# Local attention in a two-layer network on one NeuronCore: the stages of a step put one step apart, and the value products in a bank per block parity

## The reference, cut to what matters

```python
qkv = x @ Wqkv                               # 16 heads of 64
q = l2norm(q) * qs ; k = l2norm(k) * ksc
q = q * cos * scale + rotate_half(q) * sin * scale
k = k * cos * inv + rotate_half(k) * sin * inv
sim = einsum('bhwie,bhwje->bhwij', bq, bk2) * QK_SCALE   # windows of 32, each sees itself and the one before
attn = softmax(where(mask, -max, sim), -1)
out = einsum('bhwij,bhwje->bhwie', attn, bv2)
x = x + out @ Wo
...
a, gate = split(layernorm(x) @ W1 + b1, 2)
x = x + (a * gelu(gate)) @ W2 + b2
```

## Time and profile before

| | us |
|---|---|
| median of 3 runs | 6201.04 (6194.84 to 6217.79) |
| the profiled execution's own time | 6205.79 |
| its span, first to last instruction | 6204.0 |
| PE busy | 5057.0 (82%) |
| DVE busy | 3565.5 (57%) |
| ACT busy | 3480.0 (56%) |
| POOL busy | 2018.9 (33%) |
| mean granted TensorE clock | 0.892 of full speed |

### The profile page before, as it was taken

How to read it: one execution, slowest core, us unless ns; L and a number is a source line. 1 busy time by engine, 2 the same in 40 slices (tenths; PEclk the granted TensorE clock), 3 DMA queues, 4 the chain that set the end, 5 groups by cost and what they waited for, 6 DMA issues and landing times. The chain is left out here.

```text
span 6204.0 us, 161424 instructions
## 1 busy us (share of the span) xinstructions
PE 5057.0 (82%) x63808; PEld 2746.5 (44%) x63808; DVE 3565.5 (57%) x5172; ACT 3480.0 (56%) x10701; POOL 2018.9 (33%) x1438
## 2 busy tenths in 40 slices
PE   7888887777767888888888888888888888888887
PEld 3333333222224445545554455445545544554453
DVE  5677666333335556655666566555656565665564
ACT  3444444233225666666666666666666666666665
POOL 2122211000004444444444444344444444444441
PEclk9999998777678999999999999998999999999998
DMA  1000000000013233333333333333333333333332
GB/s 40 0 0 0 0 0 21 0 0 0 0 58 75 66 70 70 81 81 71 70 74 83 73 71 73 77 79 69 71 70 88 76 69 70 76 85 70 70 70 79
DMA packets 197293, 340.19 MB, mean 55 GB/s; under 512 B 63568, under 2 KB 63568, under 8 KB 195024
## 3 DMA queue, kind: packets, MB, share of 16 engines
q1 hardware_dynamic: 196560, 330.14, 22.5%
HBM read 34.19 MB, written 6.29 MB: 7 GB/s over the span
## 5 line engine op out<-in xcount | busy, mean ns | idle before, releaser
L376 ACT ACTIVATE c_Pb<-c_S,c_nb 128x64 f32<-128x64 f32 x3072 | 914.4, 323 | 477.9 <-DVE c_nb L665 476.4
L342 POOL TENSOR_TENSOR c_F<-c_tAB 128x1024 f32<-128x1024 f32 x384 | 905.9, 2359 | 8.8 <-DVE c_tAB L646 8.5
L646 DVE SCALAR_TENSOR_TENSOR c_tAB<-c_PA,c_WP,c_base 128x1024 f32<-128x1024 f32 x384 | 492.9, 1284 | 662.1 <-ACT c_sq L361 652.7
L330 POOL TENSOR_TENSOR c_Pb<-c_Pb,c_rs 128x512 f32<-128x512 f32 x384 | 400.0, 1042 | 1449.1 <-DVE c_rs L673 1449.1
L334 POOL TENSOR_TENSOR c_sq<-c_sq 128x512 f32<-128x512 f32 x384 | 486.6, 1267 | 1068.3 <-ACT c_sq L361 1068.3
L661 DVE COPY c_VO<-c_PB 128x512 f32<-128x512 f32 x384 | 265.2, 691 | 938.3 <-PE c_PB L479 938.3
L470 PE MATMUL c_PD<-c_sq,c 128*128 128x512 f32 x768 | 525.6, 773 | 332.7 <-DVE c_F L653 323.1
L376 ACT ACTIVATION_READ_ACCUMULATOR c_Pb<-c_S,c_nb 128x1 f32 x3072 | 665.9, 217 | 0.0
L519 PE MATMUL c_S<-c_PTs,c_VE 64*64 64x32 f32 x10752 | 442.8, 224 | 207.7 <-DVE c_PTs L679 198.9
L519 PEld LDWEIGHTS c_S<-c_PTs,c_VE 64*64 64x64 f32 x10752 | 404.8, 139 | 366.3 <-issue 366.3
L389 ACT ACTIVATE c_OT<-c_S 64x256 f32<-64x256 f32 x1536 | 542.8, 377 | 23.2 <-PE c_S L519 10.5
(11 more groups left out here) (247 smaller groups left out, 9515.2 us busy)
## 6 DMA issues: line engine op xcount, KB each, us to landing
c_QK<-c_F SPq DMA_DIRECT2D x3072, 64.0 KB, 2.0
c_VE<-c_VO SPq DMA_DIRECT2D x384, 128.0 KB, 2.6
c_VE<-c_VO SPq DMA_DIRECT2D x384, 96.0 KB
c_stage<-in_w_heads SPq DMA_DIRECT2D x24, 256.0 KB, 4.2
c_WT<-in_w_tails SPq DMA_DIRECT2D x6, 1024.0 KB, 5.9
a_W<-in_w_level SPq DMA_DIRECT2D x1, 3335.5 KB, 10.6
c_WT<-in_w_tails SPq DMA_DIRECT2D x6, 537.5 KB, 3.7
b_W<-in_w_level SPq DMA_DIRECT2D x1, 3133.0 KB, 10.2
```

The costliest lines, as they stand in the source:

```text
L330: nc.gpsimd.tensor_tensor(p, p, rs[:, n % 2, :].unsqueeze(2).broadcast_to([P, HS, KEYS]), ALU.mult).then_inc(*p_ready.up())
L342: nc.gpsimd.tensor_tensor(F[:, j % 2], tAB[:, j % 2, 0], tAB[:, j % 2, 1], ALU.add).then_inc(*rotated.up())
L376: e = nc.scalar.activation(Pb[:, n % 2, i, :], S[:, n % 2, r, c * KEYS:(c + 1) * KEYS], ACT.Exp, bias=nb[:, n % 2, r * PS + c:r * PS + c + ...
L646: nc.vector.scalar_tensor_tensor(out=tAB[:, kind, half], in0=bank[:, :].unsqueeze(1).broadcast_to([P, 2, SEQ]), scalar=WP[:, 2 * kind + ha ...
```

## The change

The same instructions are issued in another order, with the waits that belong to it. Only `out_copy` issues fewer: one instruction for four.

- **Squares.** ACT squares job j-1 in step n (`tb`) instead of job j, and after DVE's table products instead of before them. So DVE's products wait for the projection alone, and PE's next projection into a bank waits for the square. POOL's `add_squares`, PE's `sumsq`, ACT's `inverse_norm` and DVE's `finish` are all of job j-1 in step n; POOL's queue now has the rotation of a job ahead of the sum of its squares.
- **Tile.** `turn_probs(n)` and `pt_copy(n)` move into step n, at its end. `values(n-1)` stands behind `scores(n)`.
- **Value block.** `v_proj` comes ahead of the projections, between the squares of the last job and the second half of the new one in `PB`.
- **Banks.** `values` writes block b of a tile into bank b % 2 of the pair instead of bank r (r is the half of the rows), so that a whole head lies in one bank over all 128 partitions and `out_copy` takes both banks with one instruction.
- **Feed-forward.** `out_proj` is done in steps 0 and 1, four pairs each; the variance goes into a bank of `S`; `scale` and the first gate go to step 4.

```diff
@@ gpsimd, step
-                    if tj:
-                        add_squares(j, tj)
+                    if tb:
+                        add_squares(jb, tb)
                     if now:
                         normalise(n, now)
                     if tj:
                         rotate(j, tj)
@@ scalar
                 def square(j, half, turn):
-                    act.wait_ge(*projected.nth(2 * j + half + 1, turn))
+                    act.wait_ge(*prods.nth(2 * j + half + 1, turn))
...
-                    for r in range(2):
-                        for e in range(2):
-                            rows = slice(64 * (r ^ e), 64 * (r ^ e) + 64)
-                            mm = nc.scalar.activation(OT[rows, PS * side:PS * side + PS, e, 2 * i:2 * i + 2, :],
-                                                      S[rows, n % 2, r, :].rearrange("p (c j s q) -> p c j s q", c=PS, j=2, s=2)[:, :, :, e, :], ACT.Copy)
-                    mm.then_inc(*po_copied.up())
+                    nc.scalar.activation(OT[:, PS * side:PS * side + PS, :, 2 * i:2 * i + 2, :].rearrange("p c e j q -> p e c (j q)"),
+                                         S[:, n % 2, :, 0:PS * KEYS].rearrange("p e (c k) -> p e c k", c=PS), ACT.Copy).then_inc(*po_copied.up())
@@ scalar, step: now in this order
+                    if tb:
+                        square(jb, 0, tb)
+                        square(jb, 1, tb)
                     if now:
                         exp(n, now)
...
                     if tm:
                         out_copy(m, tm)
+                    if tb:
+                        inverse_norm(jb, tb)
...
@@ tensor
+                def first(j, turn):
...
+                        pe.wait_ge(*squared.nth(2 * j - 1, turn))
                     proj(j, 0, turn, PA)
+                def second(j, turn, v, tv):
+                    if tv:
+                        pe.wait_ge(*v_put.nth(v + 1, tv))
...
                     proj(j, 1, turn, PB)
...
+                def v_proj(v, turn, j, tj):
...
+                    if tj:
+                        pe.wait_ge(*squared.nth(2 * j, tj))
...
-                                mm = nc.tensor.matmul(S[out:out + 64, n % 2, r, c * TILE + WIN * b:c * TILE + WIN * b + WIN],
+                                mm = nc.tensor.matmul(S[out:out + 64, n % 2, b % 2, c * KEYS + WIN * (b // 2):c * KEYS + WIN * (b // 2) + WIN],
@@ tensor, step: now scores(n); values(n-1); v_proj; out_proj, gate 1, value 0, value 2;
   first(j); sumsq(j-1); second(j); out_proj, centre, variance, gate 0, gate 2, outer; turn_probs(n); value 1
@@ vector
-                    dve.wait_ge(*squared.nth(2 * j + half + 1, turn))
+                    dve.wait_ge(*projected.nth(2 * j + half + 1, turn))
@@ vector, step: now row_max(n); residual, scale, hidden 1; v_copy; products(j, 0); inv_sum(n); hidden 0, hidden 2;
   products(j, 1); pt_copy(n); finish(j-1); finish_turn; shift
```

More of the change, by code:

```diff
@@ L414, in step @@
                 def step(n, now, nxt, prev, new, fresh):
-                    j, tj = job(n, now, nxt)
                     jb, tb = job_before(n, now, nxt)
                     m, tm = back(n, 1, now, prev)
[L418 to L421, removed]
                     if tb:
[L423 to L428, removed]
+                        square(jb, 0, tb)
+                        square(jb, 1, tb)
                     if now:
                         exp(n, now)
-                    if prev and n == 4:
+                    if prev and n == 5:
                         gate_copy(1, prev)
@@ L456, in both @@
                     if j or not turn.first:
-                        pe.wait_ge(*prods.nth(2 * j, turn))
+                        pe.wait_ge(*squared.nth(2 * j - 1, turn))
                     proj(j, 0, turn, PA)
[L460 to L463, removed]
+                def second(j, turn, v, tv):
+                    if tv:
+                        pe.wait_ge(*v_put.nth(v + 1, tv))
+                    elif j:
+                        pe.wait_ge(*squared.nth(2 * j, turn))
                     proj(j, 1, turn, PB)
@@ L536, in centre, with variance @@
                     nc.tensor.matmul(PC[:, :], const.cen, x1s[:, 0:SEQ], start=True, stop=True).then_inc(*cen_done.up())
-                def variance(turn):
+                def variance(turn, now):
+                    if now:
+                        pe.wait_ge(*exps.nth(4, now))
                     pe.wait_ge(*csq_ready.nth(1, turn))
-                    nc.tensor.matmul(PA[:, :], ones_mean, csq[:, :], start=True, stop=True).then_inc(*var_done.up())
+                    nc.tensor.matmul(S[:, 1, 1, :], ones_mean, csq[:, :], start=True, stop=True).then_inc(*var_done.up())
                 def gate(c, turn):
@@ L616, in step @@
                         if n == 3:
+                            variance(prev, now)
+                        if n == 4:
                             gate(0, prev)
-                            pe.wait_ge(*lnv.nth(1, prev))
-                        if n == 4:
+                        if n == 5:
                             gate(2, prev)
-                        if n == 6:
-                            value(1, prev)
+                        if n == 7:
+                            outer(prev)
+                    if now:
+                        turn_probs(n, now)
+                    if prev and n == 6:
+                        value(1, prev)
                 turns(pe, step)
@@ L732, in step @@
                     v, tv = v_unit(n, now, nxt)
-                    m, tm = back(n, 1, now, prev)
                     if new is not None and n == 2:
                         take_scales(new)
+                    if now:
+                        row_max(n, now)
+                    if prev and n == 2:
+                        residual(prev)
+                    if prev and n == 4:
+                        scale(prev)
                     if prev and n == 7:
                         hidden(1, prev)
+                    if tv:
+                        v_copy(v, tv)
                     if tj:
@@ L740, in step @@
                     if now:
-                        row_max(n, now)
-                    if tm:
-                        pt_copy(m, tm)
-                    if prev and n == 2:
-                        residual(prev)
+                        inv_sum(n, now)
+                    if prev and n == 6:
+                        hidden(0, prev)
                     if prev and n == 7:
```

80 lines of the change are left out of this document (33 added, 47 removed).

## The result

The changed kernel took **5721.68 us** (median of 4 runs, 5717.73 to 5728.74) against 6209.41 (6194.84 to 6232.8) for the one before, run beside it: ratio 0.9213, 95% interval 0.918 to 0.9245. The forecast was 5637, with 5450 to 5970 as its range: right in its direction and inside the range, 85 us short of the gain. The profiled execution took 5723.99, 481.8 less than that of before.

A forecast was written before the change was run, and what follows sets the result against it. No engine is full; about 22 of 88.7 us a turn are waits or half clock. Steps sum to 76.7 us a turn, 12.0 less; 47 turns save 564 of 6205.8, and 4.8 for the median gives 5637 us, range 5450 to 5970.

The forecast's parts named there:

- Plain step and tile ring: One step walked from row maximum to next row maximum, through exps, first product, reciprocal, normalising, transposes, copy and finishing: 7.36 us.
- Step 2: Residual now ahead of the value copy and first product, which ends at 3.85 instead of 3.45: 7.75 us.
- step 5: Second gate stands ahead of the first projection and puts the product at 4.4: 8.3 us.
- steps 7, 0 and 1: PE binds: 9.3 us to the start of step 0's scores, then 10.1 for step 0 and 9.7 for step 1.
- switches of weights: Step 0, with four output projections on PE: 0.3 us of its 10.1.
- Step 6: ACT's gelu block delays squares and exps; PE's value projection waits, idling 3.6 us, then half clock: 14.0 us.
- The 1.8 us for half clock: Step 6: added for the value projection and the matmul behind it, after PE's idle 3.6 us.
- the key ring: A job's copies, then rotation, addition, sum, projection, second product, copy, finish: 15.25 us for two steps; step 3 7.9 us.
- first rival: Half clock in two of steps 2 to 5: 83.7 us a turn, 5966 us in all; chance 0.14.
- The ring's first term: A finished job's eight DMAs: last issued 4.35 us after the first, landing 2.0 later, 6.35 in all.
- Step 4: The scaling, two instructions about as long as the residual, pushes in ahead of the first product: 7.7 us.
- Banks in turns: Rival: value products of both row halves in one bank take turns, 2.12 us instead of 1.06; 5985 us, chance 0.06.

The follow-up runs named there:

- squares_same_step: Changed kernel with ACT squaring each job in its own step and the table products waiting for the squares again: 6147.89 us, ratio 0.9911 to the kernel before.
- gelu_last: Changed kernel with the last job's two squares issued on ACT ahead of the gelu block instead of behind it: 5594.27 us, ratio 0.9014 to the kernel before.
- shuffle_first: Changed kernel with SyncE issuing a finished job's copies ahead of the shifted values: 5680.23 us, ratio 0.9139 to the kernel before.
- three_buffers: Changed kernel with a third buffer in `F` for rotated keys and queries, three normalisation tiles kept in one: 5752.41 us, ratio 0.9262 to the kernel before.
- no_shift_of_norm: Changed kernel without the second instruction of `scale`, the addition of the shift b: 5718.22 us, ratio 0.9199 to the kernel before.
- thin_division: Changed kernel dividing only 16 of 512 columns of each new weight piece in the loop over layers, loads kept: 5718.7 us, ratio 0.92 to the kernel before.

## Why the prediction was right, and where it fell short

- **Plain step and tile ring: right.** Step 2 came out at 7.98 (forecast 7.75), step 5 at 8.02 (8.3), steps 7, 0 and 1 at 30.9 (31.0). That the walk rested on the squares leaving the products' way is shown by squares_same_step. The 30.9 is in part luck: in the 30 ordinary turns these steps take 30.1, the three pieces 9.3, 10.1 and 9.7 being 8.98, 9.78 and 9.43, and longer turns at a change of layer lift the mean. No row or run shows the 0.3 that step 0 has for the switches of weights.
- **Step 6: right**, 13.97 for 14.0, with its half clock. The prediction named the squares behind the gelu block as the cause, and gelu_last took it away. The 1.8 us for half clock are 0.90 on the value projection (1.98 for 1.08) and 0.95 on the matmul behind it (2.07 for 1.12, as it ran in gelu_last).
- **Step 3, "the key ring, with the variance on PE: 7.9": wrong, 9.06.** The step that failed is the walk itself: it counted the copies of a job as due at a rotation two steps on. For job 7 they are due earlier, at the scores of step 4, and PE waits 1.7 us in the mean for them (51.8 us in 31 waits), where the prediction, against its first rival, had holes under 1.5 us. The ring's first term was mis-sized too: issue and landing took 7.05 instead of 6.35, and the first issue came 0.50 late behind the shifted values. shuffle_first takes 0.84 us of this away, and step 3 falls to 8.19. That the rotation is not the place is shown by three_buffers.
- **Step 4, "7.7": wrong, 9.02.** Of the 1.3 us, 0.5 stand in the 8 turns at half clock behind PE's wait of step 3 (10.45 us). This is the first rival, half clock in more steps, in one step and one turn of six. The five turns with new weights (11.10) make 0.4. The rest is a plain step 4 of 8.2 us (median), of which 0.2 go with the addition of `b` (8.0 in no_shift_of_norm). What makes the last 0.3 stays open.
- **Turns that differ: left out.** The forecast took 47 equal turns of 12.0 gain. Ordinary ones gave 89.11 - 77.47 = 11.6, those with new weights 5.7, the first of a layer 11.7, the second 5.7. Over turns 1 to 46 that misses 30 x 0.4 + 5 x 6.3 + 5 x 0.3 + 6 x 6.3 = 83 us, against the 82 us that the profiled execution fell short of 564. The start of the part gained 11 us more than counted, its end lost 11, which cancels by luck. Luck is also in the ordinary turn, 77.5 us for 76.7: step 3 is 1.3 over its forecast and step 4 is 0.9 over, but steps 7, 0 and 1 are 0.9 under, step 6 is 0.3 and step 5 0.2 under.
- **Banks in turns: refuted.** By starts the value products of a tile, with both row halves in one bank, take 1.07 us in the changed kernel (the rows from 2919.60 to 2920.67 above), as the prediction's 1.06 had it; taking turns would have made 2.12. The Trainium skill, "TensorEngine Tiling (Array Packing)", Restrictions and Gotchas, would have had the other; these runs do not bear it out for products that write disjoint partitions.
- **A slip in the sums.** The inner range, 5529 to 5764, takes off the 4.8 us between the profiled execution and the median twice; 5534 to 5769 would have been right. Nothing hangs on it.
- **Signs named beforehand.** "A rotation that waits over 3 us" came (3.51) and meant nothing. "Clock rows near half outside step 6" and "a hole on PE anywhere but in step 6" came in steps 3 and 4, and mark the miss.

## What to carry to other kernels

When a pipeline is shifted, list for every transfer the earliest reader, not the usual one: here jobs 3 and 7 are read by PE one step after they are finished and the others later, and behind job 7 that step is too short for the copies. A wait off the critical path, even a long one, says nothing until it is removed, and removing it can gather its time into one longer hole ahead of TensorE, which is paid again in clock. And turns at a change of layer are worth their own line in the sum.

## What the hardware showed that was not expected

**Three DVE instructions that read and write SBUF stood still beside POOL.** They are the addition of `b`, and the cast and the subtraction of thin_division. The addition of `b` in `scale` took 485 to 488 ns in all 48 turns before, and 487 to 1295 ns, median 1214, after the change moved it beside POOL's addition. DVE, then POOL:

```profile
2948.70 1.20 DVE L693 TENSOR_SCALAR c_xn<-c_xn,c_WT 128x512 f32<-128x512 f32 x1
```

```profile
2948.33 1.28 POOL L334 TENSOR_TENSOR c_sq<-c_sq 128x512 f32<-128x512 f32 x1
```

The 16 columns of thin_division show that it is a stop and not a slower rate: 1.70 and 1.21 us for almost no data, each ending when POOL's instruction ends. The Trainium skill, "SBUF — State Buffer", Who interferes with whom, says the same of casts and scalar operations in their two-port modes and of two inputs from SBUF: the two engines share a pair of ports, and it is an exclusive lock, not a throttle. The instructions that read PSUM kept their times: the row maximum took 0.68 to 0.69 us before and after, the first table product 1.28.

**A new pass through the loop over layers begins with PE idle.** In the four turns behind a jump back to the loop's start (9, 17, 25 and 33) PE stands idle twice with nothing to wait for ("issue"): 1.2 to 1.7 us ahead of the first scores, and 1.2 to 1.3 us in the middle of the next value products. The granted clock then falls to half, and step 0 lasts 15.5 to 16.1 us instead of 10.23. Turn 1, which enters the loop from above, has no such wait and a step 0 of 12.1 us at full clock; turn 41, behind the loop, has a step 0 of 10.2. These make the 14.20 us in the mean of the six second turns. Before the change PE had one such wait at each jump, 1.4 to 2.0 us, and step 0 behind it lasted at most 10.2. PE in one of these turns, and a stretch of it, changed kernel:

```profile
2591.96 0.38 PE L493 MATMUL c_S<-c 128*128 128x256 bf16 x2 [1.68 <-issue]
...
2596.50 1.97 PE L481 MATMUL c_PB<-c_WV,xf 128*64 128x256 f32 x8
```

```profile
2594.00:2598.00 4.00, 3.35 (x67) 2.54 (x66) 0.47 (x1) 2.97 (x17) 0.00 (x0) 0.50 0.39 88
```

No run took the loop apart, so that the jump back is the cause is only argued.
